# Loading the two basis chunks of a pair with one transfer

## The chip, the cores and the metric

The kernel runs on one core of a Trainium2 chip. The metric is the device time of one execution in microseconds (us); the time before is the median of three runs. The profile is of one further execution.

## The reference, cut to what matters

A two-layer relational graph layer on 10000 nodes of 512 features with 5000 edges, followed by a mixture-of-experts block. What the change touches is how the weights of each relation are formed from 30 basis matrices:

```python
def rgcn_gate_layer(x, row, col, edge_type, basis, att, gate_w, root, bias):
    w = jnp.einsum('rb,bio->rio', att, basis)      # basis (30, 512, 512), att (2, 30)
    x_j = x[col]
    ...                                            # per relation r: sigmoid(x_j @ gate_w[r]) * x_j @ w[r]
    agg = jax.ops.segment_sum(msg, row, num_segments=x.shape[0])
    return agg + x @ root + bias                   # called twice, once per layer
```

The rest is two layer norms, the node products `x @ root` of both layers, and the experts. All matrix products are made of three float32r products each (high by high, low by high, high by low).

## The kernel before, in words

The program is written by hand per engine; each engine runs its own list of instructions in order, and semaphores tie the lists together. The phases follow each other: A (node tiles of layer 1: norm, transpose, product with root1), B (edges of layer 1), late A, C (node tiles of layer 2), D (edges of layer 2), late C, and then the groups of the experts. A node tile is 128 rows; `walk` runs eight tiles written out, a loop of eight tiles a turn, and the rest written out.

Under phases A and C, one chunk of the relation weights is formed every second tile (`w_step` names the chunk at odd tiles). The basis of a layer (31.5 MB) is seen as 120 rows (30 bases by 4 parts of the input dimension) of 128 rows `i` with 512 outputs. One chunk is four of these `i` for all 120 rows: 120 partitions by 4 by 512 floats, 960 KB. There are 32 chunks a layer (CS = 32), in 16 pairs. Of the eight `i` of a pair the even ones are chunk 0 and the odd ones chunk 1, so a chunk's reads are runs of 2 KB.

`basis_t` holds two chunks, one in each half (`basis_t[:, c, j, :]`). `load_basis` (L558 to L567) loads one chunk with two DMAs (112 partitions and the 8 left), and counts them on the semaphore of that half (`s_bin[c]`). SP runs it in its `step`: at each odd tile it waits until TensorE has formed chunk c (`s_w`), then asks for chunk c + 2 into the half just freed. At every second odd tile it then stores the formed rows of a pair (`store_w`, L578: four DMAs from `wevac`, 16 partitions by 2 KB each, into one 32 KB run of `w_dram` each). At even tiles SP asks for a pair of node tiles four pairs ahead (`load_pair`, L556: xin) and stores a finished pair (`store_pair`, L643: y or z from yout). All of these are on SP's queue, in this order.

TensorE's `w_rows` (L1275) follows the products of an odd tile: it waits for the chunk's semaphore, and four matmuls (120 by 32 weights, `att_block`) write 16 rows of weights each, two chunks accumulating into one bank. ACT evacuates the bank after the second chunk (`wevac`, L1018). When the last rows are stored, SP loads all weights back from `w_dram` into `wrl` (L633), 28 chunks first and then the other 4. wrl takes 16 KB runs for each of its 112 (then 16) partitions.

Layer 2 (phase C) starts with two chunks formed ahead (FORMED = [0, 2]): they are loaded after phase A (L696, at 315.64 us: four DMAs together) and formed after late A; at the start of phase C, SP loads chunks 2 and 3 between its first loads of xin. The loads of x for the experts (zr, L712) come in 8 KB runs over 128 partitions.

Of the kernel before, what the change touches and what calls it, by code (L numbers as in the profile page):

```python
# [21 lines left out]
F32 = mybir.dt.float32  # L22
# [34 lines left out]
def wait(eng, sem, value):  # L57

    if not isinstance(value, int) or value > 0:
        eng.wait_ge(sem, value)  # L60


def gnn_moe_kernel(nc, x, src, dst, etype, basis, att, gate_w, root, bias,
                   moe_gate_wT, moe_gate_b, w1T, sb1, rb1, w2T, sb2, rb2, out):
    N, H = x.shape
# [4 lines left out]
    R = att[0].shape[0]  # L70
# [12 lines left out]
    ISUB = 120 // NB  # L83
    BP = NB * ISUB
    BMAIN = BP // 16 * 16
    CS = P // 4
# [17 lines left out]
    z = nc.dram_tensor("z", (N + PW, H), F32, kind="Internal").ap()  # L104
    records = nc.dram_tensor("records", (P * ET + P * EC, 2), I32, kind="Internal").ap()
    src_rows = nc.dram_tensor("src_rows", (ET, P), I16, kind="Internal").ap()
    w_dram = [nc.dram_tensor(f"w_dram{l}", (CS // 2, 4, 2 * R * ISUB, H), F32, kind="Internal").ap() for l in range(2)]

    ctx = ExitStack()
    with ctx:  # L110
# [352 lines left out]
        def chunk_end(layer):  # L463
            return 2 * (CS - FORMED[layer])
# [85 lines left out]
        def _(sp):  # L550
# [4 lines left out]
                table = x if phase == SA else y1  # L555
                sp.dma_start(xin[:, gg.mod(4), 0:tiles, :], pair_rows(table, g, tiles)).then_inc(s_xin[gg.mod(4)], 16)  # L556

            def load_basis(layer, c):  # L558
                cg, u = c + CS * layer, c.div(2)
                rows = basis[layer].rearrange("b (s i) o -> (b s) i o", s=ISUB)\  # L560
                    .rearrange("p (u j c) o -> c p u j o", j=4, c=2)[c.mod(2)]
                for q in (slice(0, BMAIN), slice(BMAIN, BP)):
                    if u.i is None:
                        source = rows[q, u.k]
                    else:
                        source = rows[q, bass.ds(u.times(1), 1)].rearrange("p u j o -> p (u j) o")
                    sp.dma_start(basis_t[q, cg.mod(2), :, :], source).then_inc(s_bin[cg.mod(2)], 16)  # L567

            def store_w(layer, u):

                ug = u + CS // 2 * layer
                wait(sp, s_wv, ug.times(1, 1))
                for j in range(4):
                    if u.i is None:
                        dst_rows = w_dram[layer][u.k, j]
                    else:
                        dst_rows = w_dram[layer][bass.ds(u.times(1), 1), j].rearrange("u m o -> (u m) o")
                    sp.dma_start(dst_rows, wevac[32 * j:32 * j + 2 * R * ISUB, ug.mod(2), :]).then_inc(s_wst[ug.mod(2)], 16)  # L578

            def step(st):  # L580
                if st.phase == SC and st.t.i is None and st.t.k == 0:
                    scattered(sp, 0)
                    for g in range(4):
                        sp.wait_ge(s_norm, min(NT, 2 * (NG - 3 + g) + 2))
                        load_pair(SC, Pos(g))
                        if g < FORMED[1]:
                            sp.wait_ge(s_w, CS + g + 1)
                            load_basis(1, Pos(g + 2))
                    store_w(1, Pos(0))
                if st.phase == SA and st.t.i is None:  # L590
                    since = st.t.k - (ROOT2_AT - 4)
                    if since == 0:
                        sp.dma_start(stage1[:], root[1].rearrange("(k p) o -> p k o", p=P)).then_inc(s_root[1], 16)
                    if since in (8, 14):
                        load_gate(0, (since - 8) // 6)
                    if st.t.k == 72:
                        for r in range(R):
                            load_gate(1, r)
                        load_bias(1, s_gates2)
                        load_moe_small()  # L600
                    if 62 <= st.t.k < 62 + len(zero_rows[0]):
                        zero_late_row(0, st.t.k - 62)
                j = st.t.mod(2)
                c = w_step(st)
                if j == 0:

                    more = st.t.i is not None or st.g.k + 4 <= NG
                    if st.phase == SC and st.t.i is None and st.g.k + 4 == NA // 2:
                        sp.wait_ge(s_late, 16 * LATE_DMAS)
                    if more:  # L610
                        if st.phase == SA:
                            wait(sp, s_norm, st.n.times(1, 2))
                        else:
                            wait(sp, s_tp, st.T.times(1, 2))
                        load_pair(st.phase, st.g + 4)
                    if (st.t.i is not None or st.t.k > 1):
                        store_pair(st.phase, st.g + (-1))
                if c is not None:

                    if st.t.i is not None or st.t.k < chunk_end(st.layer) - 4:  # L620
                        wait(sp, s_w, c.times(1, 1))
                        load_basis(st.layer, st.t.div(2) + (FORMED[st.layer] + 2))
                    if st.t.mod(4) == 3:
                        store_w(st.layer, st.t.div(4) + FORMED[st.layer] // 2)
                if st.t.i is None and st.t.k - chunk_end(st.layer) in (-3, 1):

                    first, last = (0, EARLY) if st.t.k < chunk_end(st.layer) else (EARLY, CS)
                    for i in range(2):
                        sp.wait_ge(s_wst[i], 64 * (CS // 4 * st.layer + last // 4))
                    if st.layer:  # L630
                        sp.wait_ge(s_mm, C0)
                    rows = slice(4 * first, 4 * last)
                    sp.dma_start(wrl[rows, :, :].bitcast(F32),  # L633
                                 w_dram[st.layer].rearrange("u j (c m) o -> (u j c) m o", c=2)[rows]).then_inc(s_wl, 16)

            def store_pair(phase, g):
                gg = g + (NG + 1) * LAYER[phase]
# [19 lines left out]
            def load_bias(l, done):  # L657
                sp.dma_start(bias_b[l][:], bias[l].rearrange("(a d) -> a d", a=1).to_broadcast([P, H])).then_inc(done, 16)
# [25 lines left out]
                sp.dma_start(t[:], a.rearrange("(p c) -> p c", p=ER)).then_inc(s_edges, 16)  # L684
            load_pair(SA, Pos(1))
            load_bias(0, s_bias)
            for c in range(2):
                load_basis(0, Pos(c))
                load_pair(SA, Pos(2 + c))
            sp.wait_ge(s_const, 1)  # L690
            sp.dma_start(records[0:P * ET, :].rearrange("(p t) c -> p t c", p=P), fill_rec[:]).then_inc(s_fill, 16)

            walk(sp, SA, step)
            flush_stores(SA)
            for c in range(2):
                load_basis(1, Pos(c))  # L696
            zero_late_rows(1)
            sp.wait_ge(s_sm2, 16 * (2 + FC + 6))
            for r in range(1, 4):
# [494 lines left out]
        def _(pe):  # L1194
# [72 lines left out]

            def w_rows(c, layer):

                wait(pe, s_bin[c.mod(2)], c.div(2).times(32, 32))  # L1270
                u = (c + (-c.mod(2))).div(2)
                if c.mod(2) == 0:
                    wait(pe, s_wv, u.times(1, -1))
                for j in range(4):
                    ins = pe.matmul(wb[u.mod(2)][32 * j:32 * j + 32, :], att_block[layer][:, c.mod(2), :],  # L1275
                                    basis_t[:, c.mod(2), j, :], start=c.mod(2) == 0, stop=c.mod(2) == 1,
                                    tile_position=(0, 32 * j))
                ins.then_inc(s_w, 1)
# [607 lines left out]
```

## Time and profile before

| | us |
|---|---|
| median of three runs | 1627.95 |
| lowest and highest | 1626.67, 1628.1 |
| the profiled execution: span | 1621.2 |
| TensorE busy (PE) | 1557.5 |
| VectorE, ScalarE, GpSimd busy | 889.8, 748.1, 433.0 |
| chunks formed: first and last start | 26.1, 735.5 |

The span is from the first to the last instruction of the program. In the 40 slices of the page one slice is 40.5 us, a digit is the busy share in tenths. PEclk is the granted TensorE clock in tenths of full speed, DMA the mean busy share of 16 DMA engines. In the time line a line marked SPq is a DMA issue, with the time the queue needed to issue it; a bracket is idle time of the engine before the instruction and what ended it.

### The profile page before, as it was taken

The numbers are of one execution on the slowest core, as the hardware profiler recorded it, in microseconds if no ns is written. First come the engines' busy times: TensorE is split into PE (matmuls) and PEld (weight loads), VectorE is DVE, ScalarE is ACT, GpSimd is POOL, SyncE is SP. The second block draws the span as 40 slices with busy tenths as digits, with TensorE's granted clock in tenths as the row PEclk, the third lists the DMA queues.
The fourth block names the chain that finished last, engine by engine and source line by source line (L and its number), as shares of the span: only waits on it lengthen the run. The fifth ranks groups of instructions, "written<-read, shape, count | busy, mean of one in ns | idle before, by whom it ended". The sixth has DMA issues, their size and how long they took to land. (4 is left out here: it accounts for less than half of the span.)

```text
span 1621.2 us, 24004 instructions
## 1 busy us (share of the span) xinstructions
PE 1557.5 (96%) x7903; PEld 1203.9 (74%) x7903; DVE 889.8 (55%) x2181; ACT 748.1 (46%) x1219; POOL 433.0 (27%) x570
## 2 busy tenths in 40 slices
PE   6999999989998999999999899999999999999998
PEld 4676666777786767767888676777777777777777
DVE  5555686867742333346665356555555555655553
ACT  3333334656641112124665435555455545554552
POOL 4762232467743000000567431011001100110000
PEclk9999999999999999999999999999999999999999
DMA  8999999587758999997777683442244324422201
GB/s 227 277 283 280 301 302 313 177 214 129 126 79 232 305 285 275 277 288 220 182 131 131 113 215 69 128 105 80 79 128 101 84 78 127 103 81 78 91 27 46
DMA packets 96838, 274.25 MB, mean 169 GB/s; under 512 B 13990, under 2 KB 14004, under 8 KB 89058
## 3 DMA queue, kind: packets, MB, share of 16 engines
q1 hardware_dynamic: 72498, 204.10, 41.0%
q0 software_dynamic: 24240, 68.93, 23.1%
q8 instruction: 50, 0.82, 0.2%
q14 instruction: 50, 0.41, 0.1%
HBM read 179.82 MB, written 92.76 MB: 168 GB/s over the span
## 5 line engine op out<-in xcount | busy, mean ns | idle before, releaser
L974 ACT ACTIVATE th<-bank 128x512 fp32r<-128x512 f32 x158 | 94.5, 599 | 299.9 <-PE bank L1222 293.1
L1202 PE MATMUL bank<-tth,w1h 128*128 128x512 f32 (+1 forms) x400 | 164.8, 412 | 1.4 <-ACT gel L1120 1.4
L1202 PE MATMUL bank<-w2h,gth 128*128 128x512 f32 x395 | 158.3, 401 | 0.7 <-DVE gtl L1744 0.7
L1202 PE MATMUL bank<-ttl,w1h 128*128 128x512 f32 (+1 forms) x400 | 156.5, 391 | 0.0
L1202 PE MATMUL bank<-tth,w1l 128*128 128x512 f32 (+1 forms) x400 | 155.3, 388 | 0.0
L1202 PE MATMUL bank<-w2l,gth 128*128 128x512 f32 x395 | 154.5, 391 | 0.0
L1202 PE MATMUL bank<-w2h,gtl 128*128 128x512 f32 x395 | 153.8, 389 | 0.0
L1507 DVE SCALAR_TENSOR_TENSOR tl<-bank,th 128x512 fp32r<-128x512 f32 x79 | 54.4, 691 | 156.1 <-ACT th L974 150.2
L1202 PE MATMUL bank<-root2h,th 128*128 128x512 f32 x316 | 133.1, 421 | 6.2 <-DVE tl L1507 3.7
L1202 PE MATMUL bank<-root1h,th 128*128 128x512 f32 x316 | 132.5, 419 | 6.8 <-DVE yout L1536 5.1
L1202 PE MATMUL bank<-root2l,th 128*128 128x512 f32 x316 | 125.9, 399 | 0.0
L1202 PE MATMUL bank<-root1l,th 128*128 128x512 f32 x316 | 125.5, 397 | 0.0
L1202 PE MATMUL bank<-root2h,tl 128*128 128x512 f32 x316 | 124.7, 395 | 0.0
L1202 PE MATMUL bank<-root1h,tl 128*128 128x512 f32 x316 | 124.7, 395 | 0.0
L1536 DVE TENSOR_TENSOR yout<-bank,bias_b 128x512 f32<-128x512 f32 x152 | 103.7, 683 | 33.8 <-PE bank L1202 13.0
L935 POOL DMA_DIRECT2D zr<-z x19 | 18.1, 952 | 367.2 <-DMA zr<-in_x 364.5
L849 POOL DMA_INDIRECT gx<-y,dst_slot x42 | 45.3, 1080 | 263.1 <-ACT xn_e L994 240.4
L1510 DVE TENSOR_TENSOR tl<-bank,th 128x512 fp32r<-128x512 f32 x79 | 54.5, 690 | 96.6 <-ACT th L974 90.1
L1120 ACT ACTIVATE gel<-bank,b 128x512 f32<-128x512 f32 (+1 forms) x100 | 68.3, 683 | 72.7 <-PE bank L1202 72.7
L1235 PE MATMUL bank<-same,eh 128*128 128x256 f32 x336 | 84.3, 288 | 13.3 <-issue 9.2
L1202 PEld LDWEIGHTS bank<-w2h,gth 128*128 128x128 f32 x395 | 74.1, 188 | 20.2 <-issue 4.7
L1202 PEld LDWEIGHTS bank<-ttl,w1h 128*128 128x128 f32 x400 | 75.3, 188 | 16.5
(212 smaller groups left out, 3635.6 us busy)
## 6 DMA issues: line engine op xcount, KB each, us to landing
basis_t<-in_gnn_basis SPq DMA_DIRECT2D x64, 896.0 KB
xin<-in_x SPq DMA_DIRECT2D x39, 512.0 KB
xin<-y SPq DMA_DIRECT2D x39, 512.0 KB
zr<-in_x SPq DMA_DIRECT2D x19, 1024.0 KB, 4.9
out<-zr SPq DMA_DIRECT2D x19, 1024.0 KB, 3.9
y<-yout SPq DMA_DIRECT2D x37, 512.0 KB
zr<-z POOLq DMA_DIRECT2D x18, 1024.0 KB, 8.0
z<-yout SPq DMA_DIRECT2D x34, 512.0 KB
```

The source lines that it names most:

```text
L849: pool.indirect_dma_start(out=gx[:, e % 6, :], out_offset=None, in_=x if pr.phase == SB else y1, in_offset=bass.IndirectOffsetOnAxis(ap=ds ...
L935: pool.dma_start(zr[:, q.mod(4), 0:tiles_of(q), :], q_rows(z, q), accum_op=ALU.add).then_inc(s_zadd[q.mod(4)], 16)
L974: act.activation(th_a[:, s, :], tpb[s][:], f).then_inc(s_hi, 1)
L1120: act.activation(gel[:, u % 2, 0:n], outb[u % 2][:, 0:n], ACT.Gelu, bias=b1[:, c:c + 1]).then_inc(s_ge, 1)
L1202: ins = pe.matmul(out_ap, a(k), b(k), start=first, stop=last)
L1235: pe.matmul(o, eh[:, j, k * P:(k + 1) * P], m, start=j == 0, stop=False)
L1507: ins = dve.scalar_tensor_tensor(out=tl_a[:, s, :], in0=tpb[s][:], scalar=0.0, in1=th_a[:, s, :].bitcast(F32), op0=ALU.max, op1=ALU.subtract)
L1510: ins = dve.tensor_tensor(tl_a[:, s, :], tpb[s][:], th_a[:, s, :].bitcast(F32), ALU.subtract)
L1536: dve.tensor_tensor(target, out_bank(st)[:], bias_b[st.layer][:], ALU.add).then_inc(s_y, 1)
```

## The change

The rows of a pair are dealt out anew: chunk 0 takes the first four of the eight `i`, chunk 1 the last four. A pair's eight `i` are then one run of 16 KB for each of the 120 partitions. `load_basis_pair` loads both halves of `basis_t` at once, with two DMAs (112 and 8 partitions), each on its own semaphore. SP calls it at tiles 3, 7, 11, ... (`st.t.mod(4) == 3`) once the second chunk of the pair is formed, in place of one chunk at every odd tile. TensorE waits for both semaphores ahead of the first chunk of a pair and for none ahead of the second. `w_dram` gets another order of its dimensions, so that the rows land where they belong; each of the four stores of a pair then writes two runs of 16 KB in place of one of 32 KB. At the start, the pair 0 load stands ahead of xin pairs 2 and 3; at the start of phase C, the pair 1 load follows xin pairs 0 and 1.

```diff
--- before.py
+++ after.py
@@ -104,7 +104,7 @@
     z = nc.dram_tensor("z", (N + PW, H), F32, kind="Internal").ap()
     records = nc.dram_tensor("records", (P * ET + P * EC, 2), I32, kind="Internal").ap()
     src_rows = nc.dram_tensor("src_rows", (ET, P), I16, kind="Internal").ap()
-    w_dram = [nc.dram_tensor(f"w_dram{l}", (CS // 2, 4, 2 * R * ISUB, H), F32, kind="Internal").ap() for l in range(2)]
+    w_dram = [nc.dram_tensor(f"w_dram{l}", (CS // 2, 2, 4, R * ISUB, H), F32, kind="Internal").ap() for l in range(2)]
 
     ctx = ExitStack()
     with ctx:
@@ -555,16 +555,14 @@
                 table = x if phase == SA else y1
                 sp.dma_start(xin[:, gg.mod(4), 0:tiles, :], pair_rows(table, g, tiles)).then_inc(s_xin[gg.mod(4)], 16)
 
-            def load_basis(layer, c):
-                cg, u = c + CS * layer, c.div(2)
-                rows = basis[layer].rearrange("b (s i) o -> (b s) i o", s=ISUB)\
-                    .rearrange("p (u j c) o -> c p u j o", j=4, c=2)[c.mod(2)]
-                for q in (slice(0, BMAIN), slice(BMAIN, BP)):
+            def load_basis_pair(layer, u):
+                rows = basis[layer].rearrange("b (s i) o -> (b s) i o", s=ISUB).rearrange("p (u m) o -> p u m o", m=8)
+                for i, q in enumerate((slice(0, BMAIN), slice(BMAIN, BP))):
                     if u.i is None:
                         source = rows[q, u.k]
                     else:
-                        source = rows[q, bass.ds(u.times(1), 1)].rearrange("p u j o -> p (u j) o")
-                    sp.dma_start(basis_t[q, cg.mod(2), :, :], source).then_inc(s_bin[cg.mod(2)], 16)
+                        source = rows[q, bass.ds(u.times(1), 1)].rearrange("p u m o -> p (u m) o")
+                    sp.dma_start(basis_t[q].rearrange("p c j o -> p (c j) o"), source).then_inc(s_bin[i], 16)
 
             def store_w(layer, u):
 
@@ -572,9 +570,9 @@
                 wait(sp, s_wv, ug.times(1, 1))
                 for j in range(4):
                     if u.i is None:
-                        dst_rows = w_dram[layer][u.k, j]
+                        dst_rows = w_dram[layer][u.k, :, j]
                     else:
-                        dst_rows = w_dram[layer][bass.ds(u.times(1), 1), j].rearrange("u m o -> (u m) o")
+                        dst_rows = w_dram[layer][bass.ds(u.times(1), 1), :, j].rearrange("u c m o -> (u c) m o")
                     sp.dma_start(dst_rows, wevac[32 * j:32 * j + 2 * R * ISUB, ug.mod(2), :]).then_inc(s_wst[ug.mod(2)], 16)
 
             def step(st):
@@ -583,9 +581,9 @@
                     for g in range(4):
                         sp.wait_ge(s_norm, min(NT, 2 * (NG - 3 + g) + 2))
                         load_pair(SC, Pos(g))
-                        if g < FORMED[1]:
-                            sp.wait_ge(s_w, CS + g + 1)
-                            load_basis(1, Pos(g + 2))
+                        if g == FORMED[1] - 1:
+                            sp.wait_ge(s_w, CS + FORMED[1])
+                            load_basis_pair(1, Pos(1))
                     store_w(1, Pos(0))
                 if st.phase == SA and st.t.i is None:
                     since = st.t.k - (ROOT2_AT - 4)
@@ -617,9 +615,9 @@
                         store_pair(st.phase, st.g + (-1))
                 if c is not None:
 
-                    if st.t.i is not None or st.t.k < chunk_end(st.layer) - 4:
+                    if st.t.mod(4) == 3 and (st.t.i is not None or st.t.k < chunk_end(st.layer) - 4):
                         wait(sp, s_w, c.times(1, 1))
-                        load_basis(st.layer, st.t.div(2) + (FORMED[st.layer] + 2))
+                        load_basis_pair(st.layer, st.t.div(4) + (FORMED[st.layer] // 2 + 1))
                     if st.t.mod(4) == 3:
                         store_w(st.layer, st.t.div(4) + FORMED[st.layer] // 2)
                 if st.t.i is None and st.t.k - chunk_end(st.layer) in (-3, 1):
@@ -631,7 +629,7 @@
                         sp.wait_ge(s_mm, C0)
                     rows = slice(4 * first, 4 * last)
                     sp.dma_start(wrl[rows, :, :].bitcast(F32),
-                                 w_dram[st.layer].rearrange("u j (c m) o -> (u j c) m o", c=2)[rows]).then_inc(s_wl, 16)
+                                 w_dram[st.layer].rearrange("u c j m o -> (u c j) m o")[rows]).then_inc(s_wl, 16)
 
             def store_pair(phase, g):
                 gg = g + (NG + 1) * LAYER[phase]
@@ -684,16 +682,15 @@
                 sp.dma_start(t[:], a.rearrange("(p c) -> p c", p=ER)).then_inc(s_edges, 16)
             load_pair(SA, Pos(1))
             load_bias(0, s_bias)
+            load_basis_pair(0, Pos(0))
             for c in range(2):
-                load_basis(0, Pos(c))
                 load_pair(SA, Pos(2 + c))
             sp.wait_ge(s_const, 1)
             sp.dma_start(records[0:P * ET, :].rearrange("(p t) c -> p t c", p=P), fill_rec[:]).then_inc(s_fill, 16)
 
             walk(sp, SA, step)
             flush_stores(SA)
-            for c in range(2):
-                load_basis(1, Pos(c))
+            load_basis_pair(1, Pos(0))
             zero_late_rows(1)
             sp.wait_ge(s_sm2, 16 * (2 + FC + 6))
             for r in range(1, 4):
@@ -1267,8 +1264,10 @@
 
             def w_rows(c, layer):
 
-                wait(pe, s_bin[c.mod(2)], c.div(2).times(32, 32))
                 u = (c + (-c.mod(2))).div(2)
+                if c.mod(2) == 0:
+                    for i in range(2):
+                        wait(pe, s_bin[i], u.times(16, 16))
                 if c.mod(2) == 0:
                     wait(pe, s_wv, u.times(1, -1))
                 for j in range(4):
```

## Rows read from the trace of the kernel before

**Rows 1.** The page: span, busy time by engine, and lines of the 40 slices.
```profile
span 1621.2 us, 24004 instructions
...
PE 1557.5 (96%) x7903; PEld 1203.9 (74%) x7903; DVE 889.8 (55%) x2181; ACT 748.1 (46%) x1219; POOL 433.0 (27%) x570
...
DMA  8999999587758999997777683442244324422201
```

**Rows 2.** Windows, the chunk-forming stretches: busy us of engines, clock, DMA share, GB/s.
```profile
27.00:255.00 228.00, 223.13 (x1169) 157.04 (x1165) 141.16 (x344) 87.97 (x137) 92.49 (x168) 0.99 1.00 285
516.00:723.00 207.00, 206.83 (x1100) 146.72 (x1093) 72.30 (x114) 42.38 (x74) 5.70 (x6) 1.00 0.99 289
```

**Rows 3.** TensorE's waits, 27 to 303 and 515 to 740: us, times, longest.
```profile
PE bank L1202 <- DVE yout L1536: 5.1, 4, 2.0
PE bank L1222 <- ACT xn_a L966: 3.5, 7, 0.7
...
PE bank L1202 <- DVE yout L1536: 0.2, 1, 0.2
```

**Rows 4.** Time line, 101 to 119 us: start, duration; three chunks, basis issues on SP.
```profile
101.74 1.06 PE L1275 MATMUL bank<-basis_t,att_block 120*32 120x512 f32 x8
...
103.02 0.88 SPq L567 DMA_DIRECT2D basis_t<-in_gnn_basis  x2
...
109.30 1.06 PE L1275 MATMUL bank<-basis_t,att_block 120*32 120x512 f32 x8
...
110.56 0.82 SPq L567 DMA_DIRECT2D basis_t<-in_gnn_basis  x2
...
116.86 1.06 PE L1275 MATMUL bank<-basis_t,att_block 120*32 120x512 f32 x8
```

**Rows 5.** DMA issues: count, KB each, median us from issue to landing (where known).
```profile
zr<-in_x SPq DMA_DIRECT2D x19, 1024.0 KB, 4.9
...
wrl<-w_dram SPq DMA_DIRECT2D x2, 1792.0 KB, 15.7
...
zr<-in_x SPq DMA_DIRECT2D x1, 768.0 KB, 4.2
```

**Rows 6.** Four basis DMAs issued together, and windows while their data run.
```profile
315.64 2.31 SPq L567 DMA_DIRECT2D basis_t<-in_gnn_basis  x4
...
319.00:327.00 8.00, 8.00 (x47) 7.04 (x47) 7.26 (x22) 5.49 (x10) 6.13 (x5) 1.00 1.06 279
...
319.00:320.00 1.00, 1.00 (x10) 1.00 (x10) 0.96 (x6) 0.60 (x1) 0.35 (x1) 1.00 1.02 381
```

**Rows 7.** What SP issued ahead of wrl, and windows over the wrl load.
```profile
254.44 0.99 SPq L567 DMA_DIRECT2D basis_t<-in_gnn_basis  x2
...
258.29 0.36 SPq L633 DMA_DIRECT2D wrl<-w_dram  x1
...
264.50:265.50 1.00, 1.00 (x6) 0.83 (x5) 0.92 (x2) 0.98 (x3) 0.87 (x1) 1.00 1.21 328
...
266.50:267.50 1.00, 1.00 (x8) 0.89 (x7) 0.57 (x3) 0.96 (x4) 0.13 (x1) 1.00 1.06 246
```

**Rows 8.** TensorE after idle times (brackets), and windows with the granted clock.
```profile
501.78 1.06 PE L1222 MATMUL bank<-ident,xin 128*128 128x128 f32 x8 [2.39 <-DMA xin<-y]
503.95 0.77 PE L1202 MATMUL bank<-root2h,th 128*128 128x512 f32 x1 [1.10 <-issue]
...
507.07 0.43 PE L1202 MATMUL bank<-root2h,tl 128*128 128x512 f32 x1
...
510.49 1.05 PE L1222 MATMUL bank<-ident,xin 128*128 128x128 f32 x4 [2.06 <-DMA xin<-y]
...
505.00:507.00 2.00, 2.00 (x6) 1.59 (x5) 0.00 (x0) 0.00 (x0) 0.00 (x0) 0.50 1.03 270
...
273.49 0.47 PE L1202 MATMUL bank<-root1h,th 128*128 128x512 f32 x1 [1.97 <-DVE yout L1536]
...
274.00:277.00 3.00, 2.49 (x12) 1.75 (x11) 2.00 (x5) 0.82 (x1) 1.46 (x4) 1.00 1.04 411
```

## The prediction

> **What bounds the kernel now.** I read the page first: TensorE is busy for 1557.5 us of a span of 1621.2 us [rows 1]. What lengthens TensorE's own sequence lengthens the run. The DMA digits stand at 9 mostly in two stretches [rows 1], and these are the two in which basis chunks are loaded. The windows over them (27 to 255 us and 516 to 723 us) show the 16 DMA engines at a share of 0.99 to 1.00 and 285 to 289 GB/s while TensorE is busy for 223.13 of 228 us and 206.83 of 207 us, at a granted clock of 0.99 and 1.00 [rows 2]. So DMA just keeps up, and TensorE sets the pace. The waits confirm it: in the first stretch TensorE waited 5.1 us for yout and 3.5 us for xn_a, in the second 0.2 us, and for a basis chunk never [rows 3].
>
> The time line shows why it never waits. The four products that form a chunk (L1275) start at 101.74, 109.30 and 116.86 us, every 7.56 us, that is once in two node tiles. SP asks for the chunk after next in the half just freed 1.26 to 1.28 us after such a start (103.02, 110.56) [rows 4]. With two halves, a chunk asked for at 103.02 is first needed at 116.86: 13.84 us for 960 KB.
>
> **The change part by part.** *The request moves and doubles.* Both halves of basis_t are now one destination, so the pair can be asked for only when its second chunk has been formed (the 109.30 products, SP at 110.56), and the next even chunk, now waiting for the whole pair, is due at 116.86 [rows 4]. The lead is 116.86 - 110.56 = 6.30 us for 1920 KB (1.966 MB), in place of 13.84 us for 960 KB. TensorE takes instructions in order: behind the waiting products stand the next tile's transposes and matmuls, so the whole wait is added, and ACT, DVE and the stores follow later by as much. If L is the time from issue to landing, each pair costs L - 6.30 us where that is positive.
>
> *How large is L.* No view lands a basis load, so I bound it. Low end: x comes in 8 KB runs over 128 partitions, 768 KB in 4.2 us and 1024 KB in 4.9 us [rows 5]; that is 0.7 us for each 256 KB and 2.1 us without data. 1920 KB would take 4.9 + 3.5 x 0.7 = 7.35 us. Nearest in data: at 315.64 us four basis DMAs, exactly one pair's 1920 KB, are issued together. While they run (319 to 327 us) the engines are at a share of 1.06 and move 279 GB/s, 381 in the first of the eight [rows 6]. At 279 the data take 7.05 us, but the 279 includes the z rows that follow on the same queue, which engines that are done early already write; the slowest engine ends later. Nearest in shape: wrl comes over 112 partitions in 16 KB runs as the new transfer does. Its windows show 328 GB/s at first and 246 two microseconds later, at a share above 1 [rows 7], so long runs don't give the rate of the 128-partition loads. High end: wrl's 1792 KB landed 15.7 us (median of two) after the issue; counted from 254.44 us with the 2.163 MB queued ahead of it at 280 GB/s (7.7 us), 258.29 + 15.7 - 254.44 - 2.1 - 7.7 = 9.75 us are left for 1.835 MB [rows 5, 7]. At that rate 1.966 MB take 10.4 us, L = 12.5 us. I take 246 GB/s, wrl's later window, between the 279 of rows 6 and the 188 GB/s that the 9.75 us make: 8.0 us of data, L = 10.1 us, and a wait of 3.8 us. What is queued ahead (xin and y of the tile pair before, 512 KB each, issued soon after 103.02) adds nothing: 1.049 MB at 285 GB/s [rows 2] are 3.7 us, over before 110.56, since no chunk is issued at 103.02 any more.
>
> *How often.* In layer 1 pairs 1 to 15 are asked for this way (15), in layer 2 pairs 2 to 15 (14): 29 waits. Pair 0 of each layer is loaded long before. Pair 1 of layer 2 is asked for at the start of that pass, now behind two xin loads instead of between them. There TensorE waits 2.39 us and, some 8 us later, 2.06 us for xin now [rows 8]; the second should shrink as xin's second pair moves ahead of 960 KB, and the basis pair then arrives about as late for the first even chunk. I put this at nothing, with 3 us either way. 29 x 3.8 = 110 us.
>
> *The clock.* After the idle of 2.39 and 1.10 us the granted clock was at 0.50 (1.2 GHz), and the eight matmuls that started from 503.95 to 507.07 took 3.12 us for seven steps; at full clock (2.4 GHz) the same steps are half of that, so 1.5 us were lost. After an idle of 1.97 us at 273.49 the clock stayed full [rows 8]. An idle of 3.8 us is longer than both, so I charge most of 29: 1.3 us each, 38 us. Without any fall it is 0, at 1.7 for each it is 49.
>
> *What is given back.* The queue carries the same bytes in a longer time. The waits of the first stretch (8.6 us [rows 3]) may go; I take 8 us off, between 0 and 9.
>
> *The small parts.* SP issues 64 fewer basis DMAs (0.88 us for two now, [rows 4]); SP waits for TensorE there anyway, so nothing. TensorE waits for two semaphores at even chunks and none at odd ones; nothing. Nothing new is queued behind SP's wait for s_w: xin and the stores already followed it; at the first chunk of each pair they now go without it. Were that cover gone, xin would come up to 1.3 us later, against four tiles (15.1 us) of lead. The four stores of w rows go to two separate halves of 16 KB in DRAM. If all 16 engines still carry them, nothing changes. If only two do, these carry 64 KB each per pair; at a sixteenth of 280 GB/s that is 3.7 us, behind the basis pair and ahead of xin and y, hidden while the cycle has room: 262 KB per engine fill 15.0 us now; with 56 KB more it is 18.2 us, under the 15.12 + 5.1 = 20.2 us that a pair then takes.
>
> The Trainium skill ("DMA: Bandwidth & Descriptors", "Why a DMA increments its semaphore by 16 and not by 1") says that a DMA runs on the largest number of engines, up to 16, that divides the slowest dimension of both its sides. By it the stores would drop to two engines, and an 8-partition basis rest runs on eight already; no row here shows the split, and by the rule the sum stays as it is.
>
> **The sum.** 110 + 38 - 8 = 140 us on the span of 1621.2, 1761.2 us. The median of the runs, 1627.95 us, is 6.75 us over the span; I predict **1768 us**.
>
> **The rivals.** *Fast landing.* The transfer runs like the x loads: L = 7.35 us [rows 5], a wait of 1.05 us, too short for the clock to fall by rows 8. 29 x 1.05 - 8 = 22, about 1650 us. For it: the rings are free at the request. Against: both nearest loads stayed at 246 to 279 GB/s for most of their time [rows 6, 7].
>
> *Not slower.* If L stays under 6.30 + 8.6 / 29 = 6.6 us, the waits are paid by what is given back. The data would have to move in 4.5 us, 437 GB/s; the best microsecond of a basis load is 381 [rows 6]. At L = 6.5 us the result is 29 x 0.2 - 8, about 1626 us. The Trainium skill ("DMA: Bandwidth & Descriptors", "Anatomy of one DMA") fits a DMA by 2.0 us + bytes / 436e3, an estimate of 6.5 us here; the trace doesn't reach that rate for this tile.
>
> *Two slow engines.* The stores on few engines and a fast landing together: the pair's cycle would be 16.2 us against 18.2 us of work on the two engines, so these two set it: 29 x (18.2 - 15.12) - 8 = 81, about 1709 us.
>
> *Slow tail.* The 16 KB runs go as wrl's at the high end, L = 12.5 us, a wait of 6.2 us, 1.7 us of clock: 29 x 7.9 = 229, about 1857 us.
>
> **How the numbers follow.** Forecast (wait of 2.5 to 5.5 us, 1705 to 1840 us) 0.70; fast landing 0.12; two slow engines 0.05; slow tail 0.09; not slower 0.04. The range reaches from the fast landing to the top of the forecast, 1650 to 1850 us; the slow tail, half of the fast landing and the not-slower case lie outside. A measurement of this kernel tells about 0.2% from no change. Faster 0.02, same 0.02, slower 0.96.
>
> **What the profile after would show.** TensorE's waits list a wait for basis_t at L1275, some 29 times, 3 to 5 us each; TensorE's busy share falls in the two stretches and the granted clock with it; L1275 starts come 7.56 us (even to odd) and 12 to 13 us (odd to even) apart; the DMA share of these stretches falls below 0.9; everything after 723 us is only shifted. Few such waits, or ones under 1.5 us, would show the landing term wrong; waits of 4 us without a fall of the clock would show the clock term wrong; waits for xin or y in these stretches would point to the stores.

## The result, and the profile after

The changed kernel takes 1839.01 us (median of 4 runs, 1831.03 to 1842.28) against 1627.31 us of the kernel before beside it: a ratio of 1.130, 95% interval 1.126 to 1.133. The profiled execution took 1840.57 us with a span of 1838.9 us, 217.7 us more than the span of before [rows 1].

The page after: busy time, and TensorE's, the clock's and the DMA engines' lines of the 40 slices.

```profile
span 1838.9 us, 23891 instructions
...
PE 1618.1 (88%) x7903; PEld 1236.4 (67%) x7903; DVE 888.7 (48%) x2181; ACT 745.5 (41%) x1219; POOL 430.7 (23%) x570
...
PE   5777777798999777777789998999999999999999
...
PEclk9888888899999988888889999999999999999999
DMA  7666776777775866666686776933342433324211
```

The same 7903 matmuls keep TensorE busy for 1618.1 us, where it was 1557.5 [rows 1], and its share fell from 96 to 88%. The 7s of TensorE and all but two of the 8s of the clock stand where chunks are formed. The DMA line shows mostly 6s and 7s there, where it was 9s [rows 1]: the engines stand idle for a part of each pair's cycle.

TensorE's waits over the whole span (what it waited for: us in total, times, longest):

```profile
PE bank L1274 <- issue: 103.0, 19, 7.4
PE bank L1274 <- DMA basis_t<-in_gnn_basis: 61.4, 12, 5.8
...
PE bank L1199 <- DVE yout L1535: 4.7, 3, 2.0
```

L1274 is the product that forms a chunk (L1275 before). Its waits are 164.4 us in 31 times. One is the first chunk of the run (0.2 us); the other 30 are 5.5 us each. Those put down to "issue" are the same wait: each stands before an even chunk, and its end is the landing. Before there was none [rows 3]. The account closes: 164.4 us of these waits and 60.6 us of slower matmuls (1618.1 - 1557.5) are 225.0; the span grew by 217.7, so 7.3 us of other waits went.

One cycle in the time line (start, duration; in brackets the idle time before and what ended it), TensorE's and SP's lines:

```profile
102.02 1.06 PE L1274 MATMUL bank<-basis_t,att_block 120*32 120x512 f32 x8
...
103.29 0.83 SPq L565 DMA_DIRECT2D basis_t<-in_gnn_basis  x2
104.32 3.14 SPq L576 DMA_DIRECT2D w_dram<-wevac  x4
108.20 0.36 SPq L556 DMA_DIRECT2D xin<-in_x  x1
108.77 0.38 SPq L641 DMA_DIRECT2D y<-yout  x1
...
115.49 1.93 PE L1274 MATMUL bank<-basis_t,att_block 120*32 120x512 f32 x8 [5.84 <-DMA basis_t<-in_gnn_basis]
...
118.69 0.63 PE L1199 MATMUL bank<-root1h,tl 128*128 128x512 f32 x1
...
120.45 0.40 PE L1199 MATMUL bank<-root1h,th 128*128 128x512 f32 x1
...
125.12 1.06 PE L1274 MATMUL bank<-basis_t,att_block 120*32 120x512 f32 x8
```

The odd chunk is formed at 102.02, the pair asked for at 103.29. TensorE has work until 109.65 (115.49 - 5.84) and goes on when the pair is there, 12.2 us after the request. From even to odd it takes 9.63 us (115.49 to 125.12) where two tiles took 7.56 [rows 4]. The difference of 2.1 us is slower matmuls, as the windows after the wait show (busy us of PE, PEld, DVE, ACT, POOL with instructions, then granted clock, DMA share, GB/s):

```profile
116.00:119.00 3.00, 3.00 (x14) 1.55 (x7) 0.00 (x0) 0.49 (x2) 0.60 (x1) 0.50 0.57 221
121.00:124.00 3.00, 3.00 (x17) 2.48 (x16) 0.92 (x3) 1.30 (x2) 0.00 (x0) 1.00 0.43 175
```

After 5.84 us without work the granted clock is 0.50 (1.2 GHz) and then 1.00 again (2.4 GHz); the eight products of the even chunk take 1.93 us where those of the odd one take 1.06. By the trace's clock records the granted clock was 0.50 after each of the 30 waits.

The DMA issues of basis_t and of two loads to compare (KB each, median us from issue to landing):

```profile
basis_t<-in_gnn_basis SPq DMA_DIRECT2D x32, 1792.0 KB, 10.0
...
zr<-in_x SPq DMA_DIRECT2D x19, 1024.0 KB, 5.0
...
basis_t<-in_gnn_basis SPq DMA_DIRECT2D x32, 128.0 KB
...
wrl<-w_dram SPq DMA_DIRECT2D x2, 1792.0 KB, 20.8
```

The 112 partitions land 10.0 us after their issue. The last 8 partitions (128 KB, no median in the view) are a second DMA behind them. With TensorE out of work 6.36 us after the request (109.65 - 103.29) and a wait of 5.5 us, the pair is usable after 11.9 us. No view tells when the 8 partitions land, but the trace's events of their own semaphore do: the last one comes 11.7 us after the pair is asked for, 1.7 us after the last one of the 112 (medians of the 32 pairs).

### The profile page after: what moved, and what is told of

Its sections match the earlier page's. It is cut to its first block and busy times, and to the rows that moved or that the text cites. A ratio compares the mean times of both kernels' runs of the same rounds, so it can differ in the third digit from the quotient of the medians.

```text
span 1838.9 us, 23891 instructions
## 1 busy us (share of the span) xinstructions
PE 1618.1 (88%) x7903; PEld 1236.4 (67%) x7903; DVE 888.7 (48%) x2181; ACT 745.5 (41%) x1219; POOL 430.7 (23%) x570
## 5 line engine op out<-in xcount | busy, mean ns | idle before, releaser
L1274 PE MATMUL bank<-basis_t,att_block 120*32 120x512 f32 x512 | 93.9, 815 | 164.4 <-issue 103.0
L1199 PE MATMUL bank<-root1h,th 128*128 128x512 f32 x316 | 140.0, 443 | 7.1 <-DVE tl L1509 3.8
L1199 PE MATMUL bank<-root2h,th 128*128 128x512 f32 x316 | 139.0, 440 | 4.8 <-DVE tl L1506 3.5
L1274 PEld LDWEIGHTS bank<-basis_t,att_block 120*32 120x32 f32 x512 | 12.2, 122 | 188.7 <-issue 182.6
L1199 PE MATMUL bank<-root1l,th 128*128 128x512 f32 x316 | 129.9, 411 | 0.0
L1199 PE MATMUL bank<-root1h,tl 128*128 128x512 f32 x316 | 129.5, 410 | 0.0
L1199 PE MATMUL bank<-root2h,tl 128*128 128x512 f32 x316 | 129.0, 408 | 0.0
## 6 DMA issues: line engine op xcount, KB each, us to landing
xin<-in_x SPq DMA_DIRECT2D x39, 512.0 KB, 11.7
```

The lines of the kernel that those rows point to most:

```text
L1199: ins = pe.matmul(out_ap, a(k), b(k), start=first, stop=last)
```

## The experiments

Three questions: is it the lead of the request or the long runs; what makes the landing take 12 us; what would be left if the lead were long. My theory was that the lost lead makes the waits, and the waits the fall of the clock. The rival was that the 16 KB runs, or the new layout of the w rows, are themselves slow.

**The request alone** (old chunk order and runs of 2 KB, both chunks asked for at once):

```diff
-                    if st.t.i is not None or st.t.k < chunk_end(st.layer) - 4:
+                    if st.t.mod(4) == 3 and (st.t.i is not None or st.t.k < chunk_end(st.layer) - 4):
                         wait(sp, s_w, c.times(1, 1))
-                        load_basis(st.layer, st.t.div(2) + (FORMED[st.layer] + 2))
+                        for n in range(2):
+                            load_basis(st.layer, st.t.div(2) + (FORMED[st.layer] + 1 + n))
...
-                wait(pe, s_bin[c.mod(2)], c.div(2).times(32, 32))
...
+                if c.mod(2) == 0:
+                    for i in range(2):
+                        wait(pe, s_bin[i], u.times(32, 32))
```

> The request alone: both chunks of a pair are asked for together once the second chunk of the last pair is formed, with the old dealing of rows and its 2 KB runs (four DMAs of 112, 8, 112 and 8 partitions), TensorE waiting for both halves at the even chunk; w stores as before. Theory (the lead): 29 to 30 waits of 5 to 7 us at the even chunk, clock falls as in the changed kernel, 1830 to 1880 us. Rival (the 16 KB runs cost the time): waits under 2 us, below 1700 us.

It took 1831.15 us (one run). TensorE's waits:

```profile
PE bank L1280 <- issue: 106.5, 20, 7.4
PE bank L1280 <- DMA basis_t<-in_gnn_basis: 50.0, 10, 5.6
```

156.5 us in 30 waits, 5.2 us each: the request alone makes nearly the whole loss. Runs of 2 KB and of 16 KB land about equally late, so the length of the runs, which the change bought with the lead, brings nothing here.

**The runs alone** (chunk by chunk as before, but each chunk's rows dealt so that a run is 8 KB, with the w rows' new layout in DRAM):

```diff
-                    .rearrange("p (u j c) o -> c p u j o", j=4, c=2)[c.mod(2)]
+                    .rearrange("p (u c j) o -> c p u j o", j=4, c=2)[c.mod(2)]
...
-                        dst_rows = w_dram[layer][u.k, j]
+                        dst_rows = w_dram[layer][u.k, :, j]
```

> The new dealing of rows alone: a chunk is four adjacent i, read in 8 KB runs, but asked for chunk by chunk as before, with a lead of 13.84 us; the w stores go to two pieces as in the changed kernel. Theory (the shortened lead costs the time, the run length does not): no wait for basis_t, full clock, 1615 to 1632 us. Rival (long runs land slower, so the transfer itself costs the time): a chunk lands in over 13.8 us and TensorE waits for it, 1650 us or more.

It took 1641.43 us (1640.82 to 1645.48), a ratio of 1.0096 (1.0074 to 1.0118). There is no wait for the basis any more, which the lead theory wanted. But the time lies 9 us above the upper end of what I expected. TensorE's waits that are there in its place, over the whole span:

```profile
PE bank L1202 <- DVE yout L1536: 13.8, 13, 2.1
...
PE bank L1222 <- ACT xn_a L966: 7.4, 12, 2.0
```

The yout buffer is free when its y store has landed, and the store queues on SP behind what else is there. This points to the w stores, taken up below.

**The lead back, with the pair kept** (both chunks of a pair formed in one place, behind every fourth tile, so that a pair has four tiles):

```diff
-                if c is not None:
+                if c is not None and st.t.mod(4) == 3:
+                    w_rows(c + (-1), st.layer)
                     w_rows(c, st.layer)
```

> The changed kernel with one thing moved: TensorE forms both chunks of a pair behind the same tile (tiles 3, 7, 11, ...), so the pair asked for there is needed four tiles later, a lead of about 13.8 us against the 11.6 us in which it lands. Theory (the lead): no wait for basis_t over 0.5 us, clock full, 1612 to 1635 us. Rival (transfer size, or the w stores on few engines, cost the time by themselves): waits remain, above 1680 us.

It took 1677.27 us (1675.57 to 1680.78), a ratio of 1.031 (1.0287 to 1.0334). The waits for the basis are gone, and with them some 162 of the 212 us. The time is still 42 us above the upper end of what I expected. New waits took their place:

```profile
PE bank L1199 <- DVE yout L1536: 51.7, 30, 9.2
PE bank L1219 <- ACT xn_a L963: 13.8, 17, 2.9
```

Its DMA issues, the y stores:

```profile
y<-yout SPq DMA_DIRECT2D x37, 512.0 KB, 11.3
```

A y store lands 11.3 us after its issue, in the changed kernel 5.0 us.

**The clock by itself** (the changed kernel with 20 matmuls, whose result nobody reads, ahead of each wait for a pair):

```diff
                 if c.mod(2) == 0:
+                    if c.i is not None or c.k > 0:
+                        for n in range(20):
+                            pe.matmul(cnt[:], root1h[:, 0, 0:P], root1h[:, 0, :], start=True, stop=True)
                     for i in range(2):
```

> The changed kernel with 20 matmuls of 128x512 (about 0.23 us each, 4.6 us) into an unused bank ahead of each wait of an even chunk; their result is not used. They fill most of the 5.4 us wait, so the landing sets the same moment, but TensorE does not idle. Theory (the idle costs a second time, by the clock): idle before L1274 falls under 1.5 us each, the granted clock stays at 1.00 and the run takes 1770 to 1795 us, 45 to 65 us less than the changed kernel. Rival (the clock costs little and the waits are all): 1825 to 1845 us.

It took 1783.28 us (one run), 56 us less than the changed kernel although TensorE does 620 matmuls more. TensorE's waits for the pair:

```profile
PE bank L1277 <- issue: 13.8, 18, 1.4
...
PE bank L1277 <- DMA basis_t<-in_gnn_basis: 10.1, 10, 1.3
```

The window from 30 to 365 us:

```profile
30.00:365.00 335.00, 319.84 (x1618) 235.21 (x1617) 165.50 (x396) 105.30 (x165) 101.61 (x190) 1.00 0.77 226
```

It has a clock of 1.00, where the same window of the changed kernel has 0.88:

```profile
30.00:365.00 335.00, 254.67 (x1182) 174.45 (x1180) 145.62 (x353) 89.42 (x140) 96.34 (x177) 0.88 0.69 198
```

The idle time left is 23.9 us. What the clock cost is thus about 56 us by the time and 60.6 us by TensorE's busy time, 1.9 to 2.0 us for each wait.

**The order of the two DMAs** (the 8 partitions issued ahead of the 112):

```diff
-                for i, q in enumerate((slice(0, BMAIN), slice(BMAIN, BP))):
+                for i, q in ((1, slice(BMAIN, BP)), (0, slice(0, BMAIN))):
```

> The changed kernel, with the DMA of the last 8 partitions issued ahead of that of the 112. If the rest lands last only because it is queued last, the wait now ends with the 112 partitions: some 1 to 1.6 us less for each of 31 waits and a little of the clock, about 1785 to 1815 us. Rival, what counts is the bytes on the slowest engine whatever their order: the 112 partitions land as late as the rest did, 11.6 us, and the time stays at 1835 to 1842 us.

It took 1800.34 us (one run), 39 us less; the kernel before took 1621.29 us beside it, 6 us less than beside the changed kernel, so 33 to 39 us are the edit's. TensorE's waits:

```profile
PE bank L1274 <- DMA basis_t<-in_gnn_basis: 128.5, 30, 5.3
```

The view of the tile basis_t, landing of the 112 partitions:

```profile
DMA to landing us min/median/max: 9.6/10.4/19.4
```

The 30 waits shrink from 5.5 to 4.3 us. The 8 partitions were last because they were queued last: asked for first, they are there 4.2 us after the request (median, from the events of their semaphore). A fifteenth of the bytes cost 36 us of waits (164.4 - 128.5). The 112 partitions still land 10.4 us after their own issue.

**The number of partitions** (one DMA over 128 partitions, 2048 KB; source rows 240 KB apart; a row then holds 15 runs, so the last pair reads a run again):

```diff
-                rows = basis[layer].rearrange("b (s i) o -> (b s) i o", s=ISUB).rearrange("p (u m) o -> p u m o", m=8)
-                for i, q in enumerate((slice(0, BMAIN), slice(BMAIN, BP))):
+                rows = basis[layer].rearrange("b i o -> (b i) o").rearrange("(p u m) o -> p u m o", p=P, m=8)
+                for i, q in enumerate((slice(0, P),)):
...
-                        source = rows[q, u.k]
+                        source = rows[q, min(u.k, 14)]
...
-                    sp.dma_start(basis_t[q].rearrange("p c j o -> p (c j) o"), source).then_inc(s_bin[i], 16)
+                    sp.dma_start(basis_w[q].rearrange("p c j o -> p (c j) o"), source).then_inc(s_bin[i], 16)
```

> The changed kernel, but a pair comes by one DMA over 128 partitions (runs of 16 KB, 2 MB) in place of 112 partitions and a rest of 8; the products still use 120 partitions. For this the basis is read in other rows (128 runs that lie 240 KB apart), so other numbers are multiplied. If the uneven dealing of 112 and 8 partitions to the engines makes the landing long (10.0 us for the 112, 11.6 us until the rest is there): 2 MB land like the 128-partition loads of x, in about 7.5 us, a wait of 1 to 1.5 us in place of 5.4 and no half clock, so about 1650 to 1680 us. Rival, the rate of any 2 MB of this tile is what it is (245 GB/s): 8.6 + 2 us, a wait of 4.3 us, 1790 to 1830 us.

It took 1669.43 us (one run), as the theory of uneven dealing wanted. TensorE's waits, the DMA issue, and the window that begins 2 us after a request:

```profile
PE bank L1274 <- DMA basis_w<-in_gnn_basis: 49.8, 29, 3.5
```

```profile
basis_w<-in_gnn_basis SPq DMA_DIRECT2D x32, 2048.0 KB, 8.0
```

```profile
106.20:110.20 4.00, 4.00 (x21) 3.23 (x20) 2.69 (x5) 1.30 (x2) 2.89 (x3) 1.00 0.99 406
```

More bytes land in 8.0 us. The window shows 406 GB/s at a DMA share of 0.99. In the changed kernel the stretch that begins 2 us after a request, and the one behind it:

```profile
105.30:109.30 4.00, 4.00 (x21) 3.22 (x20) 2.68 (x5) 1.30 (x2) 2.88 (x3) 1.00 1.00 303
109.30:113.30 4.00, 0.35 (x2) 0.00 (x0) 0.38 (x3) 0.00 (x0) 2.71 (x6) 0.98 1.01 179
```

Its engines are as busy and move less. In the 128-partition run the waits are 1.7 us each on the mean, and TensorE is busy for 1562.7 us, 5.2 us more than in the kernel before. By the trace's clock records the granted clock stayed full after most of them; it fell to 0.50 around four, of 1.91, 2.70, 2.80 and 3.52 us, and stayed full after one of 2.18.

**The same distance of the rows, with 112 and 8 partitions**, to part the two things that the run above changed:

```diff
-                rows = basis[layer].rearrange("b (s i) o -> (b s) i o", s=ISUB).rearrange("p (u m) o -> p u m o", m=8)
+                rows = basis[layer].rearrange("b i o -> (b i) o").rearrange("(p u m) o -> p u m o", p=P, m=8)
...
-                        source = rows[q, u.k]
+                        source = rows[q, min(u.k, 14)]
```

> The changed kernel with its two DMAs of 112 and 8 partitions, but read from the same other rows of the basis as the 128-partition run (runs of 16 KB that lie 240 KB apart in place of 256 KB), so other numbers are multiplied. The 128-partition run changed two things, the partitions and the distance of the runs in DRAM; this changes the distance alone. If the dealing of 112 and 8 partitions to the engines sets the landing, nothing changes: waits of 5 to 5.6 us, 1825 to 1845 us. If it is the distance of 256 KB, the wait falls to 1.5 to 2.5 us and the time to 1665 to 1720 us.

It took 1829.51 us (one run). TensorE's waits and the DMA issue:

```profile
PE bank L1274 <- issue: 94.3, 18, 5.7
PE bank L1274 <- DMA basis_t<-in_gnn_basis: 65.7, 12, 7.4
```

```profile
basis_t<-in_gnn_basis SPq DMA_DIRECT2D x32, 1792.0 KB, 10.1
```

160.0 us of waits in 30 times, and a landing of 10.1 us. The distance of the rows in DRAM is not what made the 128-partition load fast. What is left are the partitions, and the one DMA in place of two.

**One DMA of 120 partitions**, the mend that this seemed to call for:

```diff
-                for i, q in enumerate((slice(0, BMAIN), slice(BMAIN, BP))):
+                for i, q in enumerate((slice(0, BP),)):
...
-                    for i in range(2):
-                        wait(pe, s_bin[i], u.times(16, 16))
+                    wait(pe, s_bin[0], u.times(16, 16))
```

> The changed kernel, with the pair in one DMA of 120 partitions in place of 112 and 8; rows and distance are those of the change. If the uneven dealing is what is slow (7 partitions for each of 16 engines and one more for eight of them), 8 partitions for each of 15 engines land like the 128-partition run (8.0 us): waits of 1.5 to 2.5 us, no half clock, 1665 to 1700 us. If the distance of 256 KB or the rate of the tile is: landing of 10 to 12 us, 1790 to 1850 us.

It took 1855.53 us (1853.42 to 1861.26), a ratio of 1.144 (1.140 to 1.149): slower than the change itself. The theory of uneven dealing fell, and one DMA in place of two is no help by itself. TensorE's waits, the DMA issue, and the window that begins 2 us after a request:

```profile
PE bank L1273 <- DMA basis_t<-in_gnn_basis: 178.3, 30, 6.9
```

```profile
basis_t<-in_gnn_basis SPq DMA_DIRECT2D x32, 1920.0 KB, 12.4
```

```profile
107.00:111.00 4.00, 4.00 (x21) 3.21 (x19) 2.68 (x5) 1.30 (x2) 2.88 (x3) 1.00 0.98 214
```

The window moves 214 GB/s at a share of 0.98: the engines are as busy as in the 128-partition run, at half its rate. The trace's records of single DMA packets (no view groups them; medians of three pairs from the fifth on) say the same. One run of 16 KB takes 0.62 us over 128 partitions, 0.96 to 0.99 us in the 112 and 8, and 1.23 to 1.26 us in the 120. With eight runs to an engine that is 5.0 us over 128 partitions and 10 us over 120, at the same bytes for each engine. The number of these packets that run at a time is 15 for most of the 120-partition load and 16 for most of the others. The Trainium skill ("DMA: Bandwidth & Descriptors", "Why a DMA increments its semaphore by 16 and not by 1") says that a DMA uses the largest number of engines up to 16 that divides the slowest dimension of its sides, which for 120 partitions is 15; the trace agrees on the count: 15 of the 16 steps of the load's semaphore come with the data, the first right at the issue. That a run itself becomes twice as long stands apart from that count, and why it does is open.

**The w stores.** The changed layout makes each store of 32 KB two separate pieces of 16 KB in DRAM. The split gives each piece its own DMA of 8 rows:

```diff
-                    if u.i is None:
-                        dst_rows = w_dram[layer][u.k, :, j]
...
-                    sp.dma_start(dst_rows, wevac[32 * j:32 * j + 2 * R * ISUB, ug.mod(2), :]).then_inc(s_wst[ug.mod(2)], 16)
+                    for c in range(2):
+                        if u.i is None:
+                            dst_rows = w_dram[layer][u.k, c, j]
...
+                        first = 32 * j + c * R * ISUB
+                        sp.dma_start(dst_rows, wevac[first:first + R * ISUB, ug.mod(2), :]).then_inc(s_wst[ug.mod(2)], 16)
```

In the chunk-by-chunk kernel with 8 KB runs:

> The chunk-by-chunk kernel with runs of 8 KB (1641 us, no basis waits, 21 us of yout and xn_a waits), with the same split of the stores of w rows. If the two-engine stores make those 14 us over the kernel before: 1624 to 1632 us. Rival, the chunk's own run of 8 KB or its place in the queue does it: 1638 to 1645 us as without the split.

It took 1626.2 us (1620.79 to 1630.1) beside 1621.29 us of the kernel before, a ratio of 1.0018 (1.0001 to 1.0034). In the kernel that forms both chunks in one place:

> Both chunks of a pair are formed in one place (as in the run with 1677 us, which had no wait for the basis but 51.7 us of waits for yout), and now the stores of w rows go out as eight DMAs of 8 rows with 16 KB in one piece each, in place of four with two separate pieces. If those four run on two engines only and hold back the y stores queued behind them: the yout waits fall to under 10 us and the time is 1620 to 1645 us. Rival, the y stores and xin wait behind the 1920 KB of the pair itself: 1665 to 1680 us as without the split.

It took 1656.07 us (1650.95 to 1659.11), a ratio of 1.0214 (1.0187 to 1.0241) where it was 1.031. That lies between the two cases that I had named. TensorE's waits and the DMA issue of the y stores, first of the 8 KB kernel, then of the other:

```profile
PE bank L1204 <- DVE yout L1538: 11.1, 7, 2.4
...
PE bank L1224 <- ACT xn_a L968: 5.7, 8, 2.6
```

```profile
y<-yout SPq DMA_DIRECT2D x37, 512.0 KB, 8.6
```

```profile
PE bank L1201 <- DVE yout L1538: 29.0, 21, 5.0
...
PE bank L1221 <- ACT xn_a L965: 10.1, 11, 2.9
```

```profile
y<-yout SPq DMA_DIRECT2D x37, 512.0 KB, 9.8
```

In the first the split gives back some four fifths of the 0.96%; so the stores did most of it, not the runs. In the second, about a third: the y stores land at 9.8 us in place of 11.3, and 29.0 us of yout waits stay. By the Trainium skill's rule named above ("DMA: Bandwidth & Descriptors", "Why a DMA increments its semaphore by 16 and not by 1"), the two pieces of a store would use two engines and 8 rows eight. The trace's semaphore events agree with both: three updates for each store of two pieces, where the kernel before had 13 to 15, and nine for each store of 8 rows.

**120 partitions in the kernel before, and with both chunks in one place.** The edit is that of the one DMA of 120 partitions, in the first for each chunk.

> The kernel before, with each chunk of the basis in one DMA of 120 partitions in place of 112 and 8; all else as before. If 120 partitions in one DMA land faster, the queue has more room, and the 5.1 and 3.5 us of waits for yout and xn_a in the first stretch go: 0 to 8 us less than the kernel before on the same chip. If instead 15 engines carry what 16 did where the engines were full, 960 KB more per engine cost: up to 10 us more. The first is what I expect, with little certainty.

It took 1629.37 us (1625.98 to 1634.24), a ratio of 1.0043 (1.0021 to 1.0064): 0.4% slower, the second of the two cases that I named and not the one that I expected. (The "960 KB more per engine" there is wrong: 4 KB more in each of 64 chunks are 256 KB.) Whether the 15 engines or longer runs did it, this run doesn't tell.

> Both chunks formed in one place, stores of w rows of 8 rows each (the run with 1656 us, which still waited 29.0 us for yout and 10.1 for xn_a), and the pair in one DMA of 120 partitions. If what is left there is the y stores and xin loads queued behind 10 to 12 us of pair load, a pair load of 8 us leaves less: 1630 to 1648 us. If what is left is something else (the eight products in one place, the SP issues), it stays at 1650 to 1660 us.

It took 1665.72 us (1663.3 to 1667.14), a ratio of 1.0258 (1.022 to 1.0295). That is above both cases that I had named, and the waits are longer, not shorter. The basis pair lands after 12.8 us. In the run with 112 and 8 partitions the 112 land after 10.3 us, and the whole pair after 11.8 (median, from the events of the rest's semaphore). TensorE's waits and the DMA issue:

```profile
PE bank L1201 <- DVE yout L1537: 38.9, 28, 5.7
```

```profile
basis_t<-in_gnn_basis SPq DMA_DIRECT2D x32, 1920.0 KB, 12.8
```

So the pair was there 1.0 us later, not earlier, and 9.9 us more of yout waits go with it; the two intervals of the time touch. This fits y stores queued behind the pair as what is left there, but doesn't settle it.

No version beats the kernel before. The nearest is the 8 KB runs with the split stores, at 1.0018. A second buffer for a pair, which would give the request its lead back without moving the products, wasn't tried: it needs 16 KB more in each partition, and the kernel leaves about 1.4 KB free.

## Why the prediction was right, and where its size was off

The direction, the place and the mechanism came as forecast: 1839 us lies in the range of 1650 to 1850, near its upper end and 71 us above the forecast of 1768. On the span the sum was 140 us and 217.7 came. Term by term:

- **Lead.** Forecast 6.30 us; the cycle above shows 6.36. That the request alone carries the loss, the run with 2 KB runs shows (1831 us).
- **Landing, the mis-sized term.** I took L = 10.1 us for 1920 KB as one transfer at 246 GB/s. The 112 partitions did land at 10.0. But the pair is two DMAs, and the 8 partitions behind them add some 1.7 us: waits of 5.5 us in place of 3.8. Issuing them first took 36 us off the waits. That the 112 land when I had put all 1920 KB is luck: with the 2.1 us without data taken off, their 1792 KB came at 232 GB/s and not at 246, and 1920 KB in one DMA took 12.4 us. The prediction knew of the second DMA ("an 8-partition basis rest") and gave it no time of its own. The high end, 12.5 us from the slower wrl load [rows 5, 7], was nearer to the 11.9 than the value that I took.
- **Count.** 30 waits in place of 29. Pair 1 of layer 2, put at nothing with 3 us either way, waits 7.4 us, the longest of all; the waits for xin at that place fell from 4.5 to 0.6 us. All waits together: 164.4 us measured, 110 forecast.
- **Clock, the second mis-sized term.** Forecast 1.3 us each; measured 60.6 us over 30, 2.0 each. I took it from waits of 2.39 and 1.10 us [rows 8], after which 1.5 us were lost, and scaled it down for waits that might leave the clock full. With 5.5 us the clock fell every time, and in most cases stayed at 0.50 for longer. The sign that I gave, 7.56 us from even to odd chunk, left out my own term: the slower matmuls stand there, and it was 9.63. The filler run shows that it is the clock: 56 us back with idle time filled.
- **Given back.** 8 forecast, 7.3 by the account, but in part by luck. The 8 were to be the waits for yout and xn_a in the first stretch, 8.6 us [rows 3]; of them 3.3 us, for yout, stayed. The 7.3 is what all other waits of the run lost together, those for xin among them.
- **Small parts.** The stores on few engines were seen and priced as hidden; in the changed kernel they are (4.7 us of yout waits in all), since a cycle is now longer. Where the cycle is short again they cost 0.8% (1.0096 to 1.0018) and 1.0% (1.031 to 1.021) of the kernel before, about 13 and 16 us by these ratios, 8 and 14 by the medians, each against the kernel before beside it.

The rivals. *Fast landing* needed the rate of the x loads; it exists, at 8.0 us for 2048 KB, but of the three numbers of partitions tried only for 128. The line taken from the x loads [rows 5] gives 7.7 us there. *Not slower* would have needed that rate and more; the Trainium skill's fit cited there ("DMA: Bandwidth & Descriptors", "Anatomy of one DMA") is stated for DMAs that GpSimd issues, while SP issues these. *Two slow engines* was real as a mechanism, though not what set the pace here. *Slow tail*, 1857 us, had the size nearly right: its wait of 6.2 us stands near the 5.5 measured, but the tail was the second DMA rather than a slower 112. Its sum also left out the 8 us given back, which the other rivals have; with them it is 1849 us, inside the range.

## What to carry to other kernels

A transfer that is twice as large into the same buffer waits for the last reader of both halves, so compare the lead that is left with the landing, both from the time line, before asking what the longer runs save. Of a load in several DMAs the last one issued can end the wait, here with a fifteenth of the bytes; time it by itself and try it first in the queue. And when a DRAM layout is changed to lengthen one side's runs, look at what it does to the pieces of the other side's stores and at who is queued behind them.

## What was not expected of the hardware

- The rate into SBUF went with the number of partitions, and not evenly: 2048 KB over 128 landed in 8.0 us, 1792 KB over 112 in 10.0, 1920 KB over 120 in 12.4. In the windows shown the engines were busy all the time (shares of 0.98 to 1.00), and a 16 KB run took 0.62, about 0.98 and 1.25 us. With 112 and 8 partitions, another distance of the rows in DRAM changed nothing (10.1 us); 120 partitions were not tried with it. What the cause is stays open.
- Runs of 2, 8 and 16 KB gave no difference for this tile that these runs tell: 5.2 us of wait with 2 KB, 5.5 with 16 KB, and 8 KB chunk by chunk was at 1.0018 of the kernel before once the stores were split.
- A wait of 5.5 us cost 7.5 us: 2.0 us came on top while the granted clock was at 0.50. Waits of 1.7 us on the mean, in the 128-partition run, left it at 0.99 over the run.
